# A transformer block in one kernel: expert tiles without a product for their constant rows, 71 tiles for 72, and other orders at the three seams between stages

## What is computed

```python
x = x + 0.5 * ffn(layernorm(x))
x = x + attention(layernorm(x))          # 16 heads of 8, causal, spectral-normed weights
x = x + 0.5 * ffn(layernorm(x))

# ffn: each token goes to the expert (of 8) with the largest affinity, if its rank in its batch is < cap;
# every expert is evaluated for every token, with a zero input where the mask is 0
for expert e:
    h   = gelu((inputs * mask_e) @ W1[e] + b1[e])     # 128 -> 512
    acc = acc + h @ W2[e] + b2[e]                     # 512 -> 128
```

## Time and profile before

| | us |
|---|---|
| median of 3 executions | 1034.62 (1032.22 to 1035.82) |
| the profiled execution, whole | 1035.15 |
| its span in the trace | 1033.3 |

### The profile page before, as it was taken

The page is one execution under the profiler, slowest core; times in us unless marked ns, Lnnn a source line. Parts: engine busy times, 40 slices in busy tenths (PEclk is TensorE's granted clock), DMA queues, the critical chain, the costliest instruction groups (busy, mean ns, idle before and its releaser), DMA issues. The chain is left out here.

```text
span 1033.3 us, 26499 instructions
## 1 busy us (share of the span) xinstructions
PE 896.4 (87%) x8219; PEld 679.6 (66%) x8219; DVE 724.8 (70%) x2368; ACT 607.5 (59%) x1581; POOL 682.8 (66%) x1247
## 2 busy tenths in 40 slices
PE   5937499999647999999999999999999873999995
PEld 5823399999623566565656666565656542999995
DVE  8879745444237889899998989998898845444441
ACT  2637366666313666676666666666666651766662
POOL 7709668643023678888888888888887773355554
PEclk9999799999958999999999999999999985999998
DMA  7450022223145544446354554545454102222220
GB/s 214 128 173 1 17 69 67 69 66 64 40 79 106 122 96 101 115 94 122 95 116 101 109 108 97 121 95 117 95 115 97 39 24 61 60 67 67 64 59 21
DMA packets 127407, 89.72 MB, mean 87 GB/s; under 512 B 14305, under 2 KB 117910, under 8 KB 127270
## 3 DMA queue, kind: packets, MB, share of 16 engines
q1 hardware_dynamic: 103078, 52.69, 22.8%
q10 hardware_dynamic: 15488, 17.74, 7.7%
q0 software_dynamic: 8704, 17.60, 6.6%
HBM read 52.23 MB, written 35.47 MB: 85 GB/s over the span
## 5 line engine op out<-in xcount | busy, mean ns | idle before, releaser
L1291 ACT ACTIVATE at_pt<-at_pm 128x512 f32<-128x512 f32 x384 | 228.5, 598 | 117.9 <-PE at_pm L1379 84.2
L1609 DVE TENSOR_REDUCE at_mx<-at_pp 128x2 f32<-128x512 f32 (+1 forms) x384 | 259.5, 678 | 44.7 <-PE at_pp L1368 37.1
L1207 POOL TENSOR_SCALAR_AFFINE_SELECT at_pt<-at_pt 128x256 f32<-128x256 f32 (+1 forms) x384 | 187.8, 493 | 57.4 <-ACT at_pt L1291 54.1
L925 ACT ACTIVATE e_ht<-e_ps_h,b1t 128x128 f32<-128x128 f32 x576 | 164.8, 370 | 98.2 <-PE e_ps_h L954 98.2
L964 PE MATMUL e_ps_y<-w,e_ht 128*128 x1152 | 159.2, 282 | 0.0
L954 PE MATMUL e_ps_h<-e_xnt,e_w1own 128*128 128x128 f32 x1152 | 154.8, 279 | 1.4 <-issue 1.4
L954 PEld LDWEIGHTS e_ps_h<-e_xnt,e_w1own 128*128 128x128 f32 x1152 | 143.0, 195 | 1.6 <-issue 1.6
L964 PEld LDWEIGHTS e_ps_y<-w,e_ht 128*128 128x128 f32 x1152 | 140.0, 192 | 1.7
L1011 DVE SCALAR_TENSOR_TENSOR e_y<-e_ps_y,e_x 128x256 f32<-128x256 f32 x72 | 30.6, 425 | 155.7 <-PE e_ps_y L964 155.7
L888 POOL DMA_INDIRECT out_dram<-e_y,e_x x72 | 73.6, 1022 | 86.4 <-DVE e_y L1011 74.8
L1400 PE MATMUL at_po<-at_pt,vp 128*32 128x256 f32 (+1 forms) x2048 | 109.8, 332 | 1.6 <-POOL at_pt L1207 1.6
(11 more groups left out here) (327 smaller groups left out, 1788.6 us busy)
## 6 DMA issues: line engine op xcount, KB each, us to landing
at_qkd<-at_part SPq DMA_DIRECT2D x64, 192.0 KB, 3.0
kb<-at_qkd SPq DMA_DIRECT2D x64, 96.0 KB
qs<-at_qkd ACTq DMA_DIRECT2D x64, 96.0 KB
e_x<-buckets SPq DMA_DIRECT2D x72, 66.0 KB, 1.9
x<-e_y SPq DMA_DIRECT2D x36, 128.0 KB, 1.8
rows<-ts_x ACTq DMA_DIRECT2D x16, 264.0 KB, 3.0
ts_x<-in_x_dram SPq DMA_DIRECT2D x16, 256.0 KB, 3.5
x_by_token<-at_xa SPq DMA_DIRECT2D x32, 128.0 KB
```

The lines of the kernel that those rows point to most:

```text
L925: last = a.activation(hid_t[j % NB][:, f, :], ps_h[j % NB][:, f, :], ACT.Gelu, bias=c.b1t[:, ds(e, 1), f])
L1207: g.affine_select(out=tile, in_=tile, compare_op=ALU.is_ge, fill=0.0, base=0, pattern=[[0, n], [1, P]], channel_multiplier=-1).then_inc(ma ...
L1291: a.activation(pt[u % RING][:, :], pm[u % 2], ACT.Exp, scale=SCALE).then_inc(exped, 1)
L1609: v.tensor_reduce(out, src, axis=AX.X, op=ALU.max).then_inc(maxed, 1)
```

## The change

- **No product for constant rows.** `cst`, its three parts, the split on DVE and its DMAs are gone, and the matmul L962 with them. At the head of e1 PE instead spreads the eight rows over all partitions (eight fp32 matmuls, K = 9), ACT copies them with a factor 0.5 to `c.bias`, and DVE adds the expert's row to `x_row` in place (`add_bias`, one TENSOR_TENSOR 128x128 a tile, both stages).
- **71 tiles** (`NTE = NT + E - 1`): the last pair has one tile.
- **Heads.** The first pair's two gathers of e1 move to the end of `route` on POOL, behind a semaphore on `gidx`. The first pair's two loads of e2 move to the end of `attention` on SP, behind `based`. The order of PE, ACT and DVE in the first steps is written out anew.
- **Attention's fill.** The first two gathers of attention move to the end of e1 on POOL, behind the landing of all of e1's outputs. For batch 0 the parts are written as they are made, in six DMAs, one of them on ACT's queue. In turn -1 the maxima's transposes, copy and DMA stand at step 5 and ahead of batch 2's writes. An Exp of one element at attention's start brings the table load forward. Dummy matmuls that feed nothing are added on PE: 12 at e1's end, 10 at attention's start, 8 at step 5 of turn -2, 10 at step 5 of turn -1.
- `at_p` of `route` now lies in `qs`; `base` is written before `eid`.

```diff
+NTE = NT + E - 1
+NR, HEAD_PAIRS = 8, 1
```

In `route`, on POOL:

```diff
+            pool.wait_ge(gidx_done, 1)
+            for j in range(2 * HEAD_PAIRS):
+                pool.indirect_dma_start(c.x_row[j // 2][:, j % 2, :], None, io["rows"],
+                                        bass.IndirectOffsetOnAxis(ap=c.gidx[:, j:j + 1], axis=0)).then_inc(c.x_in["e1"][j // 2], 16)
```

In `experts`, on POOL, for e1:

```diff
-                for j in range(2 * NR):
+                for j in range(2 * HEAD_PAIRS, 2 * NR):
                     gather(j)
...
+                for k in range(NR):
+                    pool.wait_ge(y_out[k], OUTS * len(range(k, NU, NR)))
+                for j in range(TPB):
+                    pool.indirect_dma_start(c.xa[0][:, j, 0:D], None, y_dram,
+                                            bass.IndirectOffsetOnAxis(ap=c.place[:, j:j + 1], axis=0)).then_inc(c.xa_in[0], 16)
```

In `experts`, on ACT:

```diff
+            if by_slot:
+                act.wait_ge(spread, 1)
+                for n in range(2):
+                    a.activation(c.bias[:, n * FC:(n + 1) * FC, :], ps_h[2 + n], ACT.Copy, scale=0.5).then_inc(bias_out, 1)
```

In `experts`, on PE (the matmul of `contract`, then the head and the end of e1):

```diff
-                te.matmul(out, c.onesb[:, :], c.cst[:, ds(e, 1), :].rearrange("p a d -> p (a d)"), start=True, stop=False)
...
+            if by_slot:
+                for n in range(E):
+                    last = te.matmul(ps_h[2 + n // FC][:, n % FC, :], c.ident[0:G, n:n + 1].to_broadcast([G, P]), c.const_rows[:, :],
+                                     start=True, stop=True, skip_group_check=True)
+                last.then_inc(spread, 1)
+            e = experts_of(pe, 0)
+            turn_x(0)
+            expand(0)
+            expand(1)
+            turn_x(1)
+            contract(0, e[0])
+            expand(2)
+            turn_x(2)
+            contract(1, e[1])
+            expand(3)
+            turn_x(3)
+            expand(4)
...
+            if by_slot:
+                for n in range(12):
+                    te.matmul(ps_h[0].rearrange("p f n -> p (f n)"), c.identb[:, :], c.mask[:, :, :].rearrange("p a q -> p (a q)"),
+                              start=True, stop=True, skip_group_check=True)
```

In `experts`, on DVE:

```diff
+            def add_bias(j, e):
+                x = x_row[(j // 2) % NR][:, j % 2, 0:D]
+                v.tensor_tensor(x, x, c.bias[:, ds(e, 1), :].rearrange("p a d -> p (a d)"), ALU.add).then_inc(biased, 1)
...
-            for j in range(FETCH):
-                fetch(j, e[j])
-            for i in range(-NORM, NU):
+            fetch(0, e[0])
+            fetch(1, e[1])
+            for i in range(NORM):
+                keep(i)
+                norm(2 * i)
+                norm(2 * i + 1)
+                if i == 0:
+                    fetch(2, e[2])
+                    fetch(3, e[3])
+                    if by_slot:
+                        dve.wait_ge(bias_out, 2)
+                if i == 2:
+                    fetch(4, e[4])
+                if i < 3:
+                    dve.wait_ge(xn_done, 2 * i + 2)
+                    add_bias(2 * i, e[2 * i])
+                    add_bias(2 * i + 1, e[2 * i + 1])
```

In `attention`: the dummy matmuls' steps, SP's writes for batch 0, SP's first loads for e2, ACT's early Exp, PE's step 5:

```diff
+        BUSY = {-4: (0, 10), -2: (5, 8), -1: (5, 10)}
...
+                    if n == 0:
+                        for done, s in ((a_done, slice(0, 6, 5)), (b_done, slice(1, 5, 3))):
+                            wait(sp, done, 1)
+                            for r in range(2):
+                                sp.dma_start(rows_out(h, r)[:, s, :], part[h][64 * r:64 * r + 64, s, :]).then_inc(piece_out, 16)
+                        wait(sp, part_done, 1)
+                        sp.dma_start(rows_out(h, 0)[:, 2:4, :], part[h][0:64, 2:4, :]).then_inc(part_out[h], 16)
+                    if b == -1:
+                        maxima_in(b, k)
...
+            for j in range(n):
+                sp.dma_start(c.x_row[j // 2][:, j % 2, :], io["buckets"][ds(r[j], P), :]).then_inc(c.x_in["e2"][j // 2], 16)
...
+            a.activation(cell[0:1, 7:8], c.part[0:1, 0:1], ACT.Exp, scale=-1.0).then_inc(early_exp, 1)
...
+                    if b in BUSY and u == BUSY[b][0]:
+                        busy(BUSY[b][1])
+                    if b == -1 and u == 5:
+                        wait(pe, r_done, b + 4)
+                        turn_maxima()
```

224 lines of the change are left out of this document (133 added, 91 removed).

## The result

The changed kernel takes 1019.67 us (median of 4 runs, 1017.70 to 1021.52), against 1034.01 us for the kernel before (4 runs): a ratio of 0.9858, 95% interval 0.9836 to 0.9880, or 14.3 us less. The forecast was 1008.0 with a range of 1002 to 1014.5, so the sign was right and 12 us of the gain did not come. The profiled execution took 1021.52 us, its span is 1019.8.

A forecast was written before the change was run, and what follows sets the result against it. PE was taken to bound both expert stages. Terms of 19.8 + 3.7 + 1.6 + 0.6 + 0.8 + 0.2 = 26.7 us took the profiled 1035.15 to 1008.4, median 1008.0, range 1002 to 1014.5.

The forecast's parts named there:

- The passes, -19.8: Both expert stages: 89 fewer PE passes each at 0.111 us, 9.9 us a stage, 19.8 us less.
- rival 1: Expert stages: the constant product's pass is worth only half, 7.9 us and not 15.9; 1016 us, chance 8%.
- rival 5: Expert stages: slower, DVE's additions and POOL block one another; 1085 us, chance 2%.
- The seam into e1, -3.7: Head of e1: earlier gathers and a higher clock make its passes start sooner; 3.7 us less, between -5.2 and +0.5.
- every engine starts e1 at about 121.9: Head of e1: the barrier waits for POOL's moved gathers, so e1 starts 2.4 us later than before.
- the ideal start at 128.3: e1: when its passes would have started if all ran at full rate, 128.3 if the clock stays low, against 132.0 before.
- The seam into attention, -1.6: From e1's last pass to attention's transposes: gathers start 1.7 us sooner; 1.6 us less, between -2.5 and +0.5.
- the slow case: Attention's start: PE's ten dummies run at the low clock, end at 286.3 and cost 1.5 us, mostly given back.
- The fill, -0.6: Attention's fill: earlier writes -0.8, dummies +0.2, the batch cycle unchanged; 0.6 us less together, from -3 to +1.
- The seam into e2, -0.8: Head of e2: two loads ahead of the barrier, expand(0) 1.2 us sooner, part lost; 0.8 us less, between -2 and +0.5.
- the end, -0.2: Kernel's end: one scatter less and faster contracts nearly cancel; 0.2 us less.
- the seams give nothing: Rival at the seams: late barrier, low-clock spread and dummies eat the gains, 19.8 and 0.8 remain; 1014 us, chance 14%.

The follow-up runs named there:

- s1_undone: The changed kernel with the gathers of e1's first pair put back into e1; 1019.11 us, 0.9853 of the time before.
- both_undone: The changed kernel with the early gathers of e1's first pair and attention's first batch back behind their barriers; 1014.88 us, 0.9817 of before.
- after_drains: The changed kernel with added POOL drains, one in e1 behind its last own gather and three in e2; 1013.17 us, 0.9786 of before.
- warm: both_undone with PE's fillers moved: 29 ahead of attention's first transposes, 9 ahead of the second, 12 ahead of the second batch's products; 1024.74 us, 0.9811.
- warm_order_again: A repeat of warm_order in another group of runs; 1023.49 us, 0.9803 of the time before.
- warm_order: warm, plus VectorE's last part ahead of the previous batch's maxima and ScalarE's batch 1 copy ahead of batch 0's reads; 1023.99 us, 0.9812.
- end_wait: both_undone with POOL waiting at e1's end for e1's outputs to land, issuing nothing behind that wait; 1029.40 us, 0.9859 of before.

## Why the prediction was wrong, point by point

- **The passes, -19.8: right.** The gap between pairs fell from 4.01 to 3.79 us, contract takes 0.89. From batch 31's scatter to e2's last `finish` it is 9.9 us less, all of one stage's term. That refutes rival 1: this kernel's passes cost 0.111 us each. With it goes half a pass, by the 56 ns of the Trainium skill, "TensorE: Matmul & The Clock Gate", section "Wait — 56ns, not 53.3ns?". `add_bias` takes 0.28 us, 0.3 forecast, and none of the 142 took more than 0.33, beside POOL's gathers too (0.28 at 160.15), so that nothing of rival 5 came; DVE is busy 27 of 50 us.
- **The seam into e1, -3.7: wrong.** The step that failed: "every engine starts e1 at about 121.9", 4.3 us behind `gidx`, with a barrier of 1.0 us taken from DVE's row. It is POOL's drain (1.8 us) and 0.7 more: 5.5 us, e1 at 124.66. That is 1.2 us more than allowed for. The second step that failed is the ideal start at 128.3, 1.3 us behind expand(0); it came 3.9 us behind it, 2.6 more. For the low clock it had 1.5 us; two expands and two transposes at 0.22 us a pass instead of 0.11 are 2.0 already by its own count, and contract(0) took 1.38 us instead of 0.89, together 2.5; and three pairs of 3.94 to 4.27 us, in no term of the sum, took 1.1; the last 0.5 us stands in no single row. Another 1.5 us of the miss is no step of it: this execution's `gidx` came at 119.12, those of s1_undone and both_undone, with the same code ahead of it, at 117.94 and 117.48. The three long pairs have a copy beside POOL's memset, as in the earlier trace rows but longer, and this time PE waits for it:

```profile
162.80 1.70 DVE L1065 COPY e_w1own<-w 128x512 f32 x1
...
164.60 1.13 PE L988 MATMUL e_ps_h<-e_xnt,e_w1own 128*128 128x128 f32 x8 [0.24 <-issue]
```

- **The seam into attention, -1.6: wrong in sign, +5.4.** The step that failed: "The barrier moves back to about 282", 5.9 us behind the last pass; it came 11.5 behind it. The forecast took 3.5 us from the outputs' landing to the start; the gathers' landing was in it, POOL's end of stage wasn't. It had been free as long as POOL finished 20 us ahead of the others; exposed, it is the drain of 71 DMAs, and with most of its account settled earlier (after_drains) the start came 7.4 behind the last pass. The gathers came as forecast, at 270.85, 2.8 us behind the last pass. The other 1.4 us of the miss lie behind the start: the transposes came 4.3 us after it and not 2.8. The normalised rows were there at 282.44, and PE stood until 283.84 in its ten fillers, which took 0.44 us each: the slow case that the forecast had priced at 1.5 and not taken.
- **The fill, -0.6: 0.0.** The reads came 5.4 us behind the first part instead of 6.4, as forecast (-0.8), and the first scores 15.9 us behind the first transposes instead of 18.1. Batch 1's scores had 1.2 us of that lead left, batch 0's scatter nothing. The step that failed is that the rest of the cycle stays as it was: the next two steps between first scores are 15.0 and 13.6 us and not 14.0 and 13.8. Batch 1's reads began at 305.30, and 8.0 us behind that, as in the kernel before, its scores could have started; PE was in ten fillers, then in the transposes of batch 0's maxima, which the change had put ahead of them:

```profile
311.68 2.68 PE L1519 MATMUL at_po<-mask,identb 128*128 128x512 bf16 x10
...
314.53 0.27 PE L1513 MATMUL at_mi<-identb,at_mp 128*48 128x128 bf16 x2 [0.17 <-POOL at_mp L1364]
```

  Where the last 1.2 us went is open.
- **The seam into e2, -0.8, and the end, -0.2:** expand(0) came 1.05 us sooner against batch 31's scatter, all of it lost again by e2's last pass; the end is 0.6 longer, five scatters queued behind PE's last passes and not four.
- **The rivals.** The second, "the seams give nothing", 1014, was the nearest and named both the barrier behind POOL's gathers and dummies in front of real work. It too held that a seam could only be eaten up; that it could cost 5 us was in no case, so the range ended at 1014.5.
- **What the profile of before could have told.** The drain's rows were there, 8.7 us at 247.9 and 8.5 at 1023.8, and so was the sign of it at the end: 7.0 us from the last scatter's end to the span's, of which the forecast took only "3.1 behind PE's end".

The page "VectorE: DVE Perf Modes" of the Trainium skill, section "The DRAIN you can't avoid", tells of a second kind of drain, boilerplate of about 12 ns on all five engines. Rows of that size stand here on four engines at a stage's last barrier (7 to 19 ns in the changed kernel; GpSimd's 34 to 41). The drains at the stage's end before it are longer: in the changed kernel's expert stages 0.33 us on VectorE, 0.81 on ScalarE, 1.6 and 3.4 on TensorE, and on GpSimd, in the stages of the table above, 1.8 to 8.2 us from its last DMA's end.

## What to carry to other kernels

An engine that ends a stage early has a hidden bill: before giving it a last task behind the others' last results, read what it does at the stage's end (its drain, under the line that opens the stage), since a wait alone exposes all of it. In the expert stages GpSimd's drain grew by 0.08 us for each DMA it had issued since its last one; a drain put where GpSimd idles took 4 us off each exposed end. In a fill, look at what stands ahead of the next batch's work in each engine's order: data that come sooner are worth nothing while a filler or another batch's work is in front of them.

## What the runs showed of the hardware

- GpSimd's drain: 5.86, 5.94 and 8.15 us behind 71, 72 and 99 DMAs that had all landed, 5.7 and 2.3 behind 69 and 24 since the last drain, 1.7 to 2.0 behind 2 to 12 with the last in flight, and 3.1 behind attention's 126, which this doesn't explain.
- PE was fully busy from 129.90 to 134.5 at half the clock. In warm it ran 29 fillers over 6.42 us and the first batch's products behind them at the full clock, and the second batch's fillers at half of it; in warm_order_again, with the same fillers and another order on ACT and VectorE, these too ran at the full clock, and in warm_order, the same kernel, they did not.
- With 28 further gathers in e1 PE idled for "issue" again and again, at a DMA share of 0.25 to 0.28, as without them (0.27 and 0.28 in end_wait). In three of the five groups PE, ACT and VectorE idled for several us at e1's head. Both are open.
